# Row normalisations of the first two batches and tiles moved from VectorE to ScalarE

## What is computed

```python
def _layernorm(x):
    return (x - mean(x)) / sqrt(var(x) + 1e-5)      # over a row of 512

x = x + xattn(_layernorm(x), ctx, ctx, Wt, Wp, Wg, Wz, gamma, beta)
x = x + ffn(_layernorm(x), w_gate, w_up, w_down)

# xattn, groups of 32 channels:
att = (Wp@q * Wg@k).sum() * 0.125;  u = Wz @ (att * Wt@v)
out = groupnorm(u) * gamma + beta + v

# ffn: q4 rounds to FP4 (E2M1) with one scale per 16 values
h = silu(q4(x) @ q4(w_gate).T) * (q4(x) @ q4(w_up).T)
out = q4(h) @ q4(w_down).T
```

## Time and profile before

| | |
|---|---|
| median of three runs | 1741.44 us (1740.36 to 1741.53) |
| span of the profiled execution | 1739.4 us |
| TensorE busy | 1682.5 us, 97% |
| VectorE busy | 1518.6 us, 87% |
| ScalarE busy | 825.6 us, 47% |
| GpSimd busy | 707.2 us, 41% |

### The profile page before, as it was taken

How to read it: one execution, slowest core, us unless ns; L and a number is a source line. 1 busy time by engine, 2 the same in 40 slices (tenths; PEclk the granted TensorE clock), 3 DMA queues, 4 the chain that set the end, 5 groups by cost and what they waited for, 6 DMA issues and landing times.

```text
span 1739.4 us, 27808 instructions
## 1 busy us (share of the span) xinstructions
PE 1682.5 (97%) x8723; PEld 922.4 (53%) x8723; DVE 1518.6 (87%) x2577; ACT 825.6 (47%) x1472; POOL 707.2 (41%) x879
## 2 busy tenths in 40 slices
PE   2789999999999999999999999999999999999999
PEld 1666555555555555555555555555555555555544
DVE  8987888889888888988888898888888988888887
ACT  3656545444445454444554444454544444545322
POOL 6865333334444333444433334443333444433310
PEclk9999999999999999999999999999999999999999
DMA  8123334334344434343434434333434444333321
GB/s 257 34 43 66 88 89 105 88 91 97 78 94 91 94 87 99 89 96 79 93 89 94 98 83 106 75 87 90 104 87 92 96 81 93 91 92 87 76 52 47
DMA packets 412150, 155.86 MB, mean 90 GB/s; under 512 B 383200, under 2 KB 384480, under 8 KB 412128
## 3 DMA queue, kind: packets, MB, share of 16 engines
q1 hardware_dynamic: 396352, 125.17, 33.7%
q10 hardware_dynamic: 15776, 30.41, 5.4%
HBM read 43.03 MB, written 16.78 MB: 34 GB/s over the span
## 4 chain that ended last, share of the span: by engine, by line
PE 94%; DVE 2%; ACT 2%; DMA 1%; issue 1%; POOL 0%; SPq 0%; DVEq 0%; ACTq 0%
PE pairs L550 52%; PE work L561 25%; PE work L500 5%; PE work L512 3%; PE ubank L527 2%; PE work L527 2%; PE pairs L605 1%; PE pairs L500 0%; PE pairs L597 0%; DMA hT_parts<-raw 0%; DMA raw<-in_L_ffn_w_gate 0%; DVE w_rinv L1205 0%; DVE x_in L1223 0%; PE pairs L607 0%; PE pairs L580 0%
## 5 line engine op out<-in xcount | busy, mean ns | idle before, releaser
L550 PE MATMUL pairs<-w_gate_hi,xT_parts 128*128 128x512 f16 (+1 forms) x1536 | 555.4, 362 | 1.8 <-DMA xT_parts<-raw 1.5
L550 PE MATMUL pairs<-w_up_hi,xT_parts 128*128 128x512 f16 (+1 forms) x1536 | 554.7, 361 | 0.0
L561 PE MATMUL work<-w_parts,hT_parts 128*128 128x512 f16 x2079 | 458.9, 379 | 0.9 <-DMA hT_parts<-raw 0.9
L561 PEld LDWEIGHTS work<-w_parts,hT_parts 128*128 128x128 f16 x2079 | 203.5, 99 | 236.1 <-issue 1.1
L550 PE MATMUL pairs<-w_up_lo,xT_parts 128*128 128x512 f16 (+1 forms) x768 | 277.5, 361 | 0.0
L550 PE MATMUL pairs<-w_gate_lo,xT_parts 128*128 128x512 f16 (+1 forms) x768 | 277.4, 361 | 0.0
L550 PEld LDWEIGHTS pairs<-w_gate_hi,xT_parts 128*128 128x128 f16 x1536 | 152.7, 99 | 163.2 <-issue 15.1
L550 PEld LDWEIGHTS pairs<-w_up_hi,xT_parts 128*128 128x128 f16 x1536 | 150.3, 98 | 146.5
L964 ACT ACTIVATE early<-pairs,w_unit 128x512 f32<-128x512 f32 (+1 forms) x192 | 124.9, 651 | 166.3 <-PE pairs L550 166.3
L873 ACT CAST raw<-hq 128x704 f16<-128x704 f32 x126 | 98.1, 779 | 179.5 <-DVE hq L1201 178.7
L1409 DVE SCALAR_TENSOR_TENSOR h<-pairs,w_unit,early 128x512 f32<-128x512 f32 (+1 forms) x192 | 135.0, 703 | 39.9 <-ACT early L964 34.6
(11 more groups left out here) (193 smaller groups left out, 2803.6 us busy)
## 6 DMA issues: line engine op xcount, KB each, us to landing
out<-raw SPq DMA_DIRECT2D x64, 256.0 KB, 2.1
c_in<-in_ctx ACTq DMA_DIRECT2D x29, 512.0 KB, 3.8
x_in<-in_x ACTq DMA_DIRECT2D x29, 512.0 KB, 5.3
raw<-in_L_ffn_w_down SPq DMA_DIRECT2D x2, 1408.0 KB, 8.9
raw<-in_L_ffn_w_gate SPq DMA_DIRECT2D x2, 1280.0 KB, 8.3
w_parts<-in_L_ffn_w_up SPq DMA_DIRECT2D x2, 1280.0 KB, 9.4
x_in<-in_x SPq DMA_DIRECT2D x3, 512.0 KB, 3.7
c_in<-in_ctx SPq DMA_DIRECT2D x3, 512.0 KB, 4.7
```

The costliest lines, as they stand in the source:

```text
L550: mm = pe.matmul(pairs[:, pair, n, 0:b - a], xT[s][part][:, k, :], w1[n][wpart][:, k, a:b], start=(k == 0 and part == 0 and wpart == 0), s ...
L561: mm = pe.matmul(obank[:, :], hT[part][:, k, :], w2[wpart][:, k, :], start=(k == 0 and part == 0 and wpart == 0), stop=(k == KH - 1 and pa ...
```

## The change

Four calls of `normalise1` (batches 0 and 1) and two of `normalise2` (tiles 0 and 1) leave VectorE. ScalarE does them as `x * rs + nm` with the Identity function, and GpSimd makes `nm = -mean * rs` in two small instructions after each inverse root. Later ones stay as they were; the first of these gets one more wait each.

```diff
@@ ScalarE
+            def early_normalise1(b, s):
+                act.wait_ge(ln1_shift, 2 * b + 2)
+                act.wait_ge(xc_ready, HT * b + s + 1)
+                nc.scalar.activation(x_in[:, s, :], x_in[:, s, :], ACT.Identity, scale=ln1_rs[:, s, 1:2],
+                                     bias=ln1_nm[:, s:s + 1]).then_inc(q_norm, 1)
+            def early_normalise2(t):
+                act.wait_ge(ln2_shift, 2 * t + 2)
+                act.wait_ge(x1_ready, t + 1)
+                at_least(act, xq_ready, t)
+                nc.scalar.activation(xn[:, :], x1[:, t % 4, :], ACT.Identity, scale=ln2_rs[:, 1:2],
+                                     bias=ln2_nm[:, 0:1]).then_inc(xn_ready, 1)
@@ ScalarE's order
             weight_grain(1)
+            early_normalise1(0, 0)
+            early_normalise1(0, 1)
             q_hi(0)
...
             weights_hi(13)
+            early_normalise2(0)
             grain_x(0)
...
             weights_lo(17)
+            early_normalise1(1, 0)
+            early_normalise1(1, 1)
             q_hi(1)
...
             weights_hi(23)
+            early_normalise2(1)
             grain_x(1)
@@ VectorE, normalise1 (normalise2 alike, with t and xn_ready)
+                if isinstance(b, int) and b < EARLY:
+                    return
+                if isinstance(b, int) and b == EARLY:
+                    dve.wait_ge(q_norm, HT * EARLY)
@@ GpSimd, ln1 (root2 alike, with one more wait on xn_ready)
+                if isinstance(b, int) and b < EARLY:
+                    pool.wait_ge(ln1_rstd, b + 1)
+                    nc.gpsimd.tensor_tensor(ln1_nm[:, :], ln1_mv[:, :, 0], ln1_rs[:, :, 1], ALU.mult).then_inc(ln1_shift, 1)
+                    pool.wait_ge(ln1_shift, 2 * b + 1)
+                    nc.gpsimd.tensor_scalar(ln1_nm[:, :], ln1_nm[:, :], -1.0, None, ALU.mult).then_inc(ln1_shift, 1)
```

More of the change, by code:

```diff
@@ L143, in build @@
         ln1_rs = sb("ln1_rs", [P, HT, 2])
+        ln1_nm = sb("ln1_nm", [P, HT])
+        ln2_nm = sb("ln2_nm", [P, 1])
+        EARLY = 2
         u_sb = sb("u_sb", [P, HT, D])
@@ L226, in build @@
         q_norm = sem("q_norm")
+        ln1_shift = sem("ln1_shift")
+        ln2_shift = sem("ln2_shift")
         q_hi_done = sem("q_hi_done")
@@ L1269, in normalise2 @@
             def normalise2(t):
+                if isinstance(t, int) and t < EARLY:
+                    return
+                if isinstance(t, int) and t == EARLY:
+                    dve.wait_ge(xn_ready, EARLY)
                 dve.wait_ge(ln2_rstd, t + 1)
@@ L1836, in root2 @@
                 inverse_root(ln2_rs[:, 1:2], ln2_rs[:, 0:1], 1, t + 1, ln2_eps, ln2_rstd)
+                if isinstance(t, int) and t < EARLY:
+                    pool.wait_ge(ln2_rstd, t + 1)
+                    at_least(pool, xn_ready, t)
+                    nc.gpsimd.tensor_tensor(ln2_nm[:, :], ln2_mv[:, 0:1], ln2_rs[:, 1:2], ALU.mult).then_inc(ln2_shift, 1)
+                    pool.wait_ge(ln2_shift, 2 * t + 1)
+                    nc.gpsimd.tensor_scalar(ln2_nm[:, :], ln2_nm[:, :], -1.0, None, ALU.mult).then_inc(ln2_shift, 1)
             def weight_y(n):
```

## The result

The changed kernel takes 1746.51 us by the median of 8 runs (1745.33 to 1747.01), the kernel before beside it 1741.49 (8 runs, 1740.36 to 1741.89). The ratio is 1.0027, 95% interval 1.0018 to 1.0036: slower by 5.0 us. The profiled execution took 1747.01 us with a span of 1745.2, 5.8 us over the span of before; it was the longest of the 8 runs.

A forecast was written before the change was run, and what follows sets the result against it. TensorE, busy 1397.76 of 1400 us from 300 to 1700 us, was taken as the bound. 1739.4 - 1.8 - 0.95 + 4.9 + 2.5 = 1744.05, with 2.04 added 1746.1 us; 8-in-10 range 1741.6 to 1748.6.

The forecast's parts named there:

- C: 117 to 125 us: x_first(1) waits for ScalarE's tile 1 normalisation, so h_done and gram(1) come late; +4.9 us.
- A: Front, 18 to 40 us: the context's reciprocal is ready earlier, ahead of weight_y(2), so gram(0) starts earlier; -1.8 us.
- 40 to 85 us rigid: Stretch of 40 to 85 us, engines handing work to and fro: taken as shifted rigidly by the front's gain.
- Rivals 3 and 4: 40 to 85 us not rigid, TensorE's 4.52 us wait shrinks: 1741.1 (0.10); also no clock fall behind 125: 1738.6 (0.05).
- The middle: 85 to 91 us, tile 0's normalisation: VectorE's saving becomes a wait for ScalarE; price 0, between -0.5 and +0.5.
- B: 101 to 109 us, batch 1: ScalarE does both halves itself, so the first silu waits only for its product; -0.95 us.
- D: Behind the gap at 125 us: TensorE's clock falls to half after idling; +2.5 us, from 0 to 3.4.
- Rival 1: TensorE's clock doesn't fall behind the gap, or for a moment only: 1743.6 us; chance 0.18.
- Rival 2: Front: ctx_power(0) still falls behind weight_y(2), so A becomes +0.3 and the time 1748.2 us; chance 0.12.
- Goes through unchanged: A shift of TensorE's instructions in the first 170 us goes through to the end unchanged.
- The 2.04 us between span and median: 2.04 us added to the summed 1744.05 us to give the forecast time of 1746.1 us.

The follow-up runs named there:

- batch 0 alone: Of the change only batch 0's two normalisations moved to ScalarE, timed beside the kernel before: 1739.23 us, ratio 0.9986.
- filled gap: The changed kernel plus 20 unused matmuls on TensorE in the gap ahead of gram(1): 1745.37 us, ratio 1.0019 against the kernel before.
- tile 1 alone: Of the change only tile 1's one normalisation moved to ScalarE, timed beside the kernel before: 1748.36 us, ratio 1.0037.
- The kernel without tile 1: The changed kernel, but tile 1's normalisation stays on VectorE at its old place: 1741.38 us, ratio 1.0002 against the kernel before.
- padding on VectorE: The whole change except tile 1's normalisation, plus one unused 128x1 VectorE instruction ahead of the loop: 1741.20 us, ratio 0.9997 against the kernel before.
- tile 1 earlier: The changed kernel with ScalarE making tile 1's normalisation right behind x_hi(0), not behind weights_hi(23): 1738.84 us, ratio 0.9983 against the kernel before.

## Why the prediction was right, and where it wasn't

The forecast was 1746.1 us, slower by 0.27%; measured were 1746.51 and 0.27%. The main term, the place of tile 1's normalisation (C), was right in its mechanism and size. That the total is within 0.4 us is in part luck: its steps add up to +4.65, of which the trace has +3.4 at the last `gram`, and a loss at the end that no step had fills the difference. By its steps:

- **A, -1.8:** measured -2.06 at `gram(0)`, and by batch 0 alone -2.06 at the last `gram` and -2.4 in the median. VectorE's L1504 (the successor of L1470) did go in front of `ctx_lo` and held it, as the step chose.
- **40 to 85 us rigid:** -2.06 at 38.5 and -1.98 at 100 us. Rivals 3 and 4 fall: the long wait at 73 us is 4.37 instead of 4.52 us.
- **The middle, 0:** VectorE starts `x_first(0)` at 84.70, 1.97 us earlier than before, like everything else; the wait is whole.
- **B, -0.95:** -0.95 in the change (2.93 less 1.98) and -0.96 alone. The 0.38 us that stay are the silu and the copy ahead of the weights.
- **C, +4.9:** 1.98 + 2.93 = +4.91. The reason, VectorE's queue behind `x_first(1)`, was shown from both sides: with the instruction earlier on ScalarE, or `gated(0, 0, 2)` earlier on VectorE, the gap is gone.
- **D, +2.5:** the step that failed, by its size. The clock fell, and it costs +1.3 (4.07 - 2.78, and 1.31 by the filled gap). The step took 5 us at half clock from the longest wait before (rows 10); here the stretch was 3.4 us, and 0.8 of it lay in the gap. With tile 1 alone it cost 1.7. Rival 1 (no fall, +0) is wrong as well; 1.3 lies midway between the two.
- **Rival 2** is out: `ctx_power(0)` is ahead of `weight_y(2)` by 0.7 us, as worked out.
- **"Goes through unchanged":** true here (+3.3 and +3.4), but not a law of this loop. TensorE's busy share of all but 100% (rows 1) hides that the transpose of `xT` lands just when TensorE is ready. The kernel without tile 1 lost 2.2 of its 3.4 us there.
- **Not foreseen:** the end. By the steps up to the loop the profile is 3.4 us later than before; 2.4 more come in the last unit. So two errors cancelled: D was 1.2 us too large, and the end cost an estimated 1.6 in the medians (5.0 less the trace's 3.4). The +2.4 belong to the profiled execution.
- **The 2.04 us between span and median:** each run on record is 1.8 to 1.9 us longer than its span (1747.01 and 1745.2). It falls out of the difference of the two kernels.

Open is why the last transpose takes about 3.1 us in some kernels and 3.7 in others, and with it what of the loss at the end the change causes. TensorE's wait for it was 1.46 to 1.67 us in the profiles of the kernel before, of batch 0, batch 1 and tile 1 alone and with padding on VectorE, 2.15 to 2.18 in seven others and in that of the change, and 3.05 with the filled gap. Wherever the clock fell there, the wait was 2.15 or more, but in two profiles (everything but tile 1, and tile 1 earlier) it was as long and the clock stayed. No run takes the cause apart.

## What to carry to other kernels

When an instruction moves to another engine, its length matters less than the two queues it joins. Look at what stands ahead of it on its new engine, and what stands behind its first consumer on the old one; here 0.8 us of work at the wrong place cost 6.8, and at a better one 0.2 at `gram(1)` (121.81 for 121.58 without the move). If TensorE can't be kept from waiting, look for a second price in the clock behind the gap: 1.3 to 1.7 us behind 4.75 here, and none where the gap was filled or came in pieces of up to 1.12 us. In a loop where two chains arrive together, compare one iteration's time before crediting an edit ahead of it.

## What the hardware showed that I had not expected

- The number of instructions that ScalarE has ahead of the loop changes how late it starts one instruction in it: 0.80 or 0.87 us from the start of VectorE's `xq` to its copy, for one tile in each iteration. Of the counts seen (216, 217, 218, 221, 222) only 221 has 0.87, in both kernels that have this count; the eight with 222 all have 0.80. One 128x1 instruction more on ScalarE switches it back, one on VectorE doesn't. Why, no trace shows.
- A VectorE instruction of 128x32 or 128x176 numbers, 0.18 or 0.19 us long, takes 2.60 or 2.31 beside GpSimd's large ones. For such waits the Trainium skill's page "SBUF — State Buffer", section "Who interferes with whom", has a VectorE instruction in a two-port mode and one of GpSimd exclude each other; these rows agree as to the wait (they don't show the mode), and show that small size is no protection.
- The price of TensorE's gap of 4.75 us in the clock was 1.3 us in one kernel and 1.7 in another, with the same half-clock stretch of 3.4 us, since its start against the gap's end differs. 20 unused matmuls brought it to nothing.
